# Masked cross attention on one NeuronCore: next-stage loads moved forward, small row transfers moved to another queue, and half of the mask additions moved from TensorE to VectorE

## The reference

```python
x = x + tanh(g_xattn[0]) * L0_attention(layernorm(x), ctx)         # attention over heads, token by token
x = x + tanh(g_ffn[0])   * L0_ffn(layernorm(x))                    # quantised feed-forward
# the stage that is changed: 16 heads of 16, queries from x, keys and values from ctx
q = layernorm(x); query = LN(q @ Wq + bq); key = LN(ctx @ Wk + bk); value = LN(ctx @ Wv + bv)
scores = einsum('bhqd,bhkd->bhqk', query, key) / sqrt(16)
scores = where(mask == 0, -1e9, scores)                            # mask is (8, 512, 512), 0 or 1
probs  = softmax(scores, axis=-1)
x = x + tanh(g_xattn[1]) * (einsum('bhqk,bhkd->bqhd', probs, value) @ Wo + bo)
x = x + tanh(g_ffn[1])   * L1_experts(layernorm(x))                # 8 experts, the best 2 for each token
```

## Time and profile before

| what | value |
|---|---|
| median of 3 runs | 2364.2 us (2363.41 to 2366.39) |
| time of the profiled execution | 2363.78 us |
| its span, first to last instruction | 2362.0 us |
| mean granted clock of PE | 0.905 |
| first_layer, from 0 to about | 553.5 us |
| cross_attention before unit 0, from there to | 682.8 us |
| units 0 to 127, from there to about | 1480 us |
| experts and the end, to | 2362.0 us |

### The profile page before, as it was taken

How to read it: one execution, slowest core, us unless ns; L and a number is a source line. 1 busy time by engine, 2 the same in 40 slices (tenths; PEclk the granted TensorE clock), 3 DMA queues, 4 the chain that set the end, 5 groups by cost and what they waited for, 6 DMA issues and landing times. The chain is left out here.

```text
span 2362.0 us, 35706 instructions
## 1 busy us (share of the span) xinstructions
PE 1962.9 (83%) x12086; PEld 1390.9 (59%) x12086; DVE 1570.8 (67%) x3184; ACT 1078.0 (46%) x2055; POOL 927.8 (39%) x679
## 2 busy tenths in 40 slices
PE   5888898875277989889898979710799999999998
PEld 3566666663123434333343424610799999999998
DVE  7999999973165656556565655450577777777775
ACT  2233334432234555546454545210465655656654
POOL 6988888852432323323232200137222222222222
PEclk8899999987678999999999989655899999999999
DMA  8000000001516345261615320242466666666662
GB/s 291 32 10 10 10 7 10 8 0 56 96 43 96 69 62 90 44 103 32 100 55 77 74 35 2 72 146 100 152 222 224 213 224 225 216 227 226 221 214 73
DMA packets 145296, 245.79 MB, mean 104 GB/s; under 512 B 12613, under 2 KB 90530, under 8 KB 145189
## 3 DMA queue, kind: packets, MB, share of 16 engines
q1 hardware_dynamic: 134540, 219.18, 35.1%
q0 software_dynamic: 10624, 25.26, 2.9%
q10 hardware_dynamic: 24, 0.01, 0.0%
HBM read 201.96 MB, written 45.76 MB: 105 GB/s over the span
## 5 line engine op out<-in xcount | busy, mean ns | idle before, releaser
L1267 DVE CUSTOM_DVE_ANT_0 x_dump<-x_ps,x_bias_q 128x512 bf16<-128x512 f32 x512 | 353.4, 690 | 198.4 <-PE x_ps L1020 185.1
L1171 ACT ACTIVATE x_PT<-x_ps 128x512 f32<-128x512 f32 x512 | 296.1, 600 | 262.9 <-PE x_ps L1035 253.5
L1034 PE MATMUL x_ps<-x_bias_k,x_ident_b 128*128 128x512 bf16 x512 | 200.9, 392 | 75.7 <-DMA x_QS<-x_rows 75.7
L1020 PE MATMUL x_ps<-x_KS,x_QS 96*128 96x512 bf16 x512 | 203.6, 400 | 30.8 <-DMA x_KS<-parts 19.3
L1787 ACT ACTIVATE e_silu<-m_ps 128x256 f32<-128x256 f32 x312 | 118.5, 380 | 232.8 <-PE m_ps L1724 232.7
L1691 POOL DMA_INDIRECT out_dram<-e_y,e_label x78 | 79.0, 1012 | 367.2 <-DVE e_y L1843 355.4
L1035 PE MATMUL x_ps<-x_QS,x_KS 98*128 98x512 bf16 x512 | 200.2, 391 | 0.0
L1826 DVE TENSOR_TENSOR e_gated<-e_silu,m_ps 128x256 f32<-128x256 f32 x312 | 120.8, 417 | 103.0 <-ACT e_silu L1787 98.5
L1724 PE MATMUL m_ps<-e_x_lo,m_hi 128*128 128x256 f32 x640 | 181.4, 283 | 1.5 <-DVE e_x_lo L1811 1.5
L1724 PE MATMUL m_ps<-e_x_hi,m_lo 128*128 128x256 f32 x640 | 181.4, 283 | 0.0
L1724 PE MATMUL m_ps<-e_x_hi,m_hi 128*128 128x256 f32 x640 | 181.1, 283 | 0.0
(11 more groups left out here) (285 smaller groups left out, 5517.7 us busy)
## 6 DMA issues: line engine op xcount, KB each, us to landing
m_raw<-in_L_ffn_w_dram SPq DMA_DIRECT2D x117, 1024.0 KB, 5.1
parts<-x_part SPq DMA_DIRECT2D x24, 512.0 KB, 2.9
x_QS<-parts SPq DMA_DIRECT2D x48, 256.0 KB, 12.0
x_KS<-parts SPq DMA_DIRECT2D x48, 256.0 KB, 16.5
expert_in<-a_blank SPq DMA_DIRECT2D x1, 10062.0 KB, 28.4
e_x<-expert_in SPq DMA_DIRECT2D x39, 258.0 KB, 5.8
x_mask_q<-in_mask_dram SPq DMA_DIRECT2D x32, 256.0 KB, 2.8
x_mask_k<-in_maskT_dram SPq DMA_DIRECT2D x32, 256.0 KB, 2.7
```

Source lines behind the costliest of these rows:

```text
L1020: pe.matmul(ps_max[m % 2], QS[b % 2][0:HROWS, h, q * P:(q + 1) * P], KS[b % 2][0:HROWS, h, :], start=True, stop=True).then_inc(s1_ps, 1)
L1034: pe.matmul(ps_st[e % 3], ident_b[:, :], bias_k[b % 2][:, kc, :], start=True, stop=False)
L1171: act.activation(PT[unit % 2][:, k, :], ps_st[e % 3], ACT.Exp, scale=DH ** -0.5).then_inc(exp_done, 1)
L1267: dve.tensor_tensor_reduce(out=dump[:, :], in0=ps_max[m % 2], in1=bias_q[b % 2][:, q, :], scale=1.0, scalar=NEG, op0=ALU.add, op1=ALU.max, ...
```

## The change

In first_layer, SP also loads the second attention's weights, scales, first two context tiles and first two mask tiles, and DVE splits its biases into three parts in round 33 of 39; all go to tiles that live through both stages (Ahead). In cross_attention:

- the loads of the weights and the bias split at the start are gone; FIRST_UNIT is -16, and start_of is two units later (4n - 28). The first four tiles have their own full and rest (in PT), and DVE does their scale_and_shift, remainder and low_part;
- the extra rows are placed by ACT's own queue, one unit later; the spreading is cut in two: the first two of eight pairs of heads, with a count of their own (first_in), then the rest; SP waits for a given rows transfer before it spreads;
- the first two heads of each group get no mask matmul (CUT = 2). After the second maximum of each unit, DVE takes the minimum of the two exponentials of the unit before and of (mask bias + 2^100), in one instruction on 128 x 1024 elements, and PE's values wait for it (cut_masked);
- once a batch, PE adds up the mask biases of all keys in ps_m, and DVE corrects the bias of those queries that keep no key (keys): one operation on 128 x 512 and four more that add to the four bias tiles; the maximum is bounded to match (NONE_KEPT).

```diff
+            for n in range(2):
+                sp.dma_start(ahead.cT[n][:, :, :], cv[:, :, n * P:(n + 1) * P]).then_inc(ahead.loaded, 16)
+            sp.dma_start(ahead.wkv[:, :, 0:D], k2(L1[2])).then_inc(ahead.loaded, 16)
...
+                if t == NT + 1:
+                    split_biases(7, next_row, next_rest, next_parts)
...
+            def place_rows(g):
+                b = g // GROUPS
+                act.wait_ge(rows_sb, g + 1)
+                heads = slice(4 * (g % GROUPS), 4 * (g % GROUPS) + 4)
+                for r in range(MROWS):
+                    act.dma_start(QS[b % 2][HROWS + r:HROWS + r + 1, heads, :], rows[4 * r:4 * r + 4, :]).then_inc(rows_in, 16)
...
                     if k == 0:
+                        if group_at(unit + 1) is not None:
+                            place_rows(group_at(unit + 1))
...
+                        if b:
+                            sp.wait_ge(rows_in, 16 * MROWS * (rows_before_spread(b) + 1))
                         for part in range(3):
-                            spread_part(b, part)
+                            spread_part(b, part, slice(0, 2), first_in)
+                        for part in range(3):
+                            spread_part(b, part, slice(2, H // 2), spread_in)
...
                 if i == 0:
+                    pe.wait_ge(first_in, 16 * 2 * PARTS * (b + 1))
+                elif i == 16:
                     pe.wait_ge(spread_in, 16 * 2 * PARTS * (b + 1))
...
-                if u == 0 and k == 0:
-                    pe.wait_ge(k_masked, TPB * (b + 1))
+                if u == 0 and k == CUT:
+                    pe.wait_ge(m_free, m_freed["keys", b])
...
-                pe.matmul(ps_st[e % 3], ident_b[:, :], bias_k[b % 2][:, kc, :], start=True, stop=False)
+                if k >= CUT:
+                    pe.matmul(ps_st[e % 3], ident_b[:, :], bias_k[b % 2][:, kc, :], start=True, stop=False)
                 pe.matmul(ps_st[e % 3], KS[b % 2][:, h, kc * P:(kc + 1) * P], QS[b % 2][:, h, :],
-                          start=False, stop=True).then_inc(st_ready, 1)
+                          start=(k < CUT), stop=True).then_inc(st_ready, 1)
...
                 pe.wait_ge(exp_done, 4 * (unit + 1))
+                pe.wait_ge(cut, unit + 1)
...
+                elif what == "keys":
+                    for kc in range(TPB):
+                        mm = pe.matmul(ps_m, ones_b[:, :], bias_k[n % 2][:, kc, :], start=(kc == 0), stop=(kc == TPB - 1))
...
+            def keys(b):
+                dve.wait_ge(m_ready, m_use["keys", b] + 1)
+                steps.done(dve.tensor_scalar(ps_m, ps_m, SEQ * NEG, NONE_KEPT - NEG, ALU.is_equal, ALU.mult))
+                steps.wait()
+                for kc in range(TPB):
+                    d = dve.tensor_tensor(bias_k[b % 2][:, kc, :], bias_k[b % 2][:, kc, :], ps_m, ALU.add)
+                d.then_inc(m_free, 1)
+
+            def cut_masked(unit):
+                b, u = divmod(unit, UNITS)
+                if u == 0:
+                    dve.wait_ge(m_free, m_freed["keys", b])
+                dve.wait_ge(exp_done, 4 * unit + CUT)
+                out = PT[unit % 2][:, 0:CUT, :]
+                dve.scalar_tensor_tensor(out=out, in0=bias_k[b % 2][:, u % TPB, :].unsqueeze(1).broadcast_to([P, CUT, SEQ]),
+                                         scalar=-NEG, in1=out, op0=ALU.add, op1=ALU.min).then_inc(cut, 1)
...
                 for m in islice(maxima, 2):
                     maximum(m)
+                if 0 <= unit - 1 < NUNITS:
+                    cut_masked(unit - 1)
                 for n in tiles_at(unit - 1):
                     kv_stats(n)
...
+                if unit == FIRST_UNIT + 4:
+                    dve.wait_ge(ahead.loaded, AHEAD)
+                    for n in range(EARLY):
+                        scale_and_shift(n)
+                        if n > 1:
+                            remainder(n - 2)
+                    for n in range(EARLY - 2, EARLY):
+                        remainder(n)
+                        low_part(n - 2)
+                    for n in range(EARLY - 2, EARLY):
+                        low_part(n)
```

More of the change, by code:

```diff
@@ L2 @@
 from concourse import mybir
+from collections import namedtuple
 from contextlib import ExitStack
@@ L640 @@
 NEG = -2.0 ** 100
+NONE_KEPT = NEG + 2.0 ** 92
+CUT = 2
 PARTS = 6
@@ L649, with middles_at, rows_before_spread @@
 Q_PARTS, K_PARTS = (0, 0, 1, 1, 0, 2), (0, 1, 0, 1, 2, 0)
-FIRST_UNIT, LAST_UNIT = -18, NUNITS + 5
+FIRST_UNIT, LAST_UNIT = -16, NUNITS + 5
 def start_of(n):
-    return FIRST_UNIT if n < EARLY else 4 * n - 30
+    return FIRST_UNIT if n < EARLY else 4 * n - 28
 def split_of(n):
-    return FIRST_UNIT + 4 + n if n < EARLY else start_of(n) + 4
+    return start_of(n) + 4
+def middles_at(unit):
+    return [n for n in range(NT) if split_of(n) + (1 if n < EARLY else 2) == unit]
 def spread_of(b):
-    return split_of(TPB * b + TPB - 1) + 3
+    return split_of(TPB * b + TPB - 1) + (3 if b else 1)
+def rows_before_spread(b):
+    return (spread_of(b) + 1) // 4
 def tiles_at(unit):
@@ L701, in bank_m_events @@
         late.append(("spread", group_at(unit - 6)))
+    if (unit + 1) % UNITS == 0 and 0 <= unit + 1 < NUNITS:
+        late.append(("keys", (unit + 1) // UNITS))
     if group_at(unit + 2) is not None:
@@ L796, in cross_attention @@
                     m_use[e], m_before[e], last = len(m_use), last, e
-                    if e[0] in ("spread", "output"):
+                    if e[0] in ("spread", "keys", "output"):
                         m_freed[e] = len(m_freed) + 2
@@ L972, in _ @@
                     q_deviations(n)
-                if unit == FIRST_UNIT + 4:
+                if unit == FIRST_UNIT + 2:
                     x_deviations(1)
@@ L1093, in _ @@
                         scores(unit, k)
-                    if k == 1:
+                    if k == (1 if unit >= 0 else 3):
                         for n in tiles_at(unit - 2):
@@ L1229, in split_bias, with part_at, scale_and_shift, remainder @@
                 dve.tensor_tensor(part(2), remainder, part(1), ALU.subtract).then_inc(bias_split, 1)
+            def part_at(n, k):
+                return parts[0][k][:, :, :, n * P:(n + 1) * P].rearrange("p k c n -> p (k c) n")
+            def scale_and_shift(n):
+                dve.wait_ge(turned, n + 1)
+                for k in range(4):
+                    d = dve.tensor_scalar(full(n)[:, k, :], bank_of(n)[:, k * P:(k + 1) * P], scale4[:, k:k + 1], shift4[:, k:k + 1],
+                                          ALU.mult, ALU.add)
+                d.then_inc(full_done, 1)
+            def remainder(n):
+                dve.wait_ge(hi_done, n + 1)
+                dve.tensor_tensor(rest(n), full(n), part_at(n, 0), ALU.subtract).then_inc(rest_done, 1)
+            def low_part(n):
+                dve.wait_ge(mid_done, n + 1)
+                dve.tensor_tensor(part_at(n, 2), rest(n), part_at(n, 1), ALU.subtract).then_inc(lo_done, 1)
             def normalise(n):
@@ L1330, in _ @@
                         divide(n)
+                    elif what == "keys":
+                        keys(n)
                     elif what == "output":
                         output(n)
-                if unit == FIRST_UNIT + 3:
+                if unit == FIRST_UNIT + 2:
                     x_stats(1)
+                if unit == FIRST_UNIT + 4:
+                    dve.wait_ge(ahead.loaded, AHEAD)
+                    for n in range(EARLY):
+                        scale_and_shift(n)
+                        if n > 1:
+                            remainder(n - 2)
+                    for n in range(EARLY - 2, EARLY):
+                        remainder(n)
+                        low_part(n - 2)
+                    for n in range(EARLY - 2, EARLY):
+                        low_part(n)
                     dve.wait_ge(rstd_done, 2)
```

212 lines of the change are left out of this document (111 added, 101 removed).

## The result

The changed kernel takes 2421.1 us, median of 4 runs (2418.76 to 2425.35); the kernel before took 2365.3 beside it on the same chip. The ratio is 1.0235, 95% interval 1.0214 to 1.0256. So the change costs 56 us, where 22 were forecast. The profiled execution took 2425.35, its span is 2423.6, so span against span the difference is 61.6 us.

What follows compares the result with a forecast made beforehand. A batch was taken as PE's, with DVE having 40 us to spare on average. Terms -43 + 1 - 81 + 3 + 78 - 1 + 10 + 3 + 24 + 28 gave +22: 2364.2 to 2386 us, range 2344 to 2422.

Steps and rivals of the forecast that it cites:

- start, with the bias split: Before unit 0: earlier loads, own tile buffers and less spreading to await give -43; bias split in first layer +1.
- rows: stall gone, what is left late: Seven PE stalls before units needing rows: -76, slower matmuls behind them -5, remaining lateness +3.
- backlog: Four-unit cycles: DVE's statistics and other work delay the first maximum, +0.4 a cycle over 26 cycles, +10 (0 to 40).
- rival 3: The stall stays: rows still queue in the transfer engines, half of 76 comes back, 2424 us; chance 0.06.
- I add 3: Rows on ACT's queue: lateness left after the later issue, +3 (0 if always landed, 10 if spreading slows it).
- The cut: PE-DVE-PE loop of plain units: 4.40 instead of 3.76 us, +78 over 122 units; about -1 in the last six.
- The port: Cut and POOL shut each other out of SBUF in a cycle's second and third units: +28 (0 to 60).
- The keys: Once a batch, five DVE operations (3.2 us) before the next unit's first maximum: 8 x 3.0, +24 (16 to 28).
- Rival 1: POOL is never in the cut's way: the port's 28 go, start at -48, rows on time, 2350; chance 0.22.
- Rival 2: PE loses its clock (1 a batch, +8) and port waits reach 2.3 a cycle (+30): 2424 us; chance 0.10.
- Rival 4: The cut is hidden, plain units 3.76 or less, so 78 + 10 + 28 go: 2270 us; chance 0.06.
- no wait of PE for the rows beyond 1 us: Sign expected in the profile after: PE never waits over 1 us for the extra rows.

Runs made afterwards that it cites:

- run 3: Changed kernel with the extra rows issued as soon as they are copied, a unit earlier, still on ACT's queue: 2402.1 us.
- run 9: Changed kernel with the rows back on SP's queue, issued two units ahead as in the kernel before: 2411.5 us.
- run 10: Kernel without keys, with spreading in four paced steps, early rows on ACT's queue, new start and the cut of two heads: 2350.9 us.
- run 11: Changed kernel with one head cut instead of two (CUT = 1): 2379.9 us.
- run 4: Changed kernel with the cut after all maxima of its own unit instead of between the maxima of the next: 2413.2 us.
- run 8: Changed kernel with POOL beginning its operations in each unit only when that unit's cut is over: 2406.5 us.
- run 2: Changed kernel without the keys event (no sums of mask biases on PE, no bias correction on DVE): 2392.9 us.
- run 6: Changed kernel with the spreading from the second batch on in four paced steps of 12 smaller transfers: 2379.9 us.
- run 7: Changed kernel without cut and keys, with paced spreading, early rows and a bound of the maxima that never acts; new start kept: 2229.0 us.

## Why the prediction came out wrong in size

The direction held, and so did the mechanisms of the start, the cut, the port and the keys; that of the rows did not. The sum was 34 short of the medians' difference. By terms, from unit starts, span against span:

| term | forecast | measured | from |
|---|---|---|---|
| start, with the bias split | -42 | -38 | unit 0 at 644.6, before 682.8 |
| rows: stall gone, what is left late | -78 | -41 | seven units and the ones behind them: 84.0 before, 43.2 after |
| all else in the loop (cut, backlog, outputs, keys, port, last units) | +142 | +142 | units 0 to 127: 100.7 longer, plus the 41 |
| end | 0 | -1 | after unit 127 |
| sum | +22 | +62 | span 2423.6 against 2362.0 |

**The rows: the step that failed.** "On ACT's queue they no longer stand behind the spreading: -76, and -5 for the slower matmuls behind seven stalls", with the 3 for lateness, was mis-sized by half; 41 came, not 78. The mechanism behind it, that a queue of one's own lets a small transfer pass, gives almost nothing here (runs 3 and 9). The prediction had drawn on the Trainium skill (DMA: Bandwidth & Descriptors, Queues, rings and completion order) for it, and the measurement does not agree: 8 KB on ACT's ring took 8.9 us with the spreading in flight, with no packet moved for the first 7.7 of them, and came when SP's own next tile came. This is rival 3 ("half of 76 comes back: 2424"), which was given 0.06 on the words "another ring". The rows of the trace had more to say. In the kernel before, the rows reached PE 31.0 after the first issue of the spreading. The change makes SP wait for the rows of unit 8 before it begins, and 31 us do not fit into four units of 22 to 26: 31 - 26 is the 5 of each stall. That sum was to be made and was not. "I add 3" priced a single small transfer, without what else is in flight, and even its upper end, "10 if the rest of the spreading slows it", is a quarter of the 43 that were left.

**The cut.** 78 - 1 + 10 + 3 + 28 = 118 was forecast, the port included, and run 10 measures 122. The two parts err in opposite directions: the port is under its 28 (below), so the rest of the cut is above its 90. That the table's third row agrees to a microsecond is partly luck. The loop of a plain unit was followed step by step: 4.46 to 4.50 against 4.40, by the cut's hand-over (0.15 instead of 0.07). Run 11 confirms that it goes by length, and run 4 that it goes by place. DVE's 1.22 alone was exact.

**The port.** The two units of a cycle were named rightly, and the two that are free of it. The size is 20.7 of longer cuts instead of 28, and 15 by removal (run 8). The lock itself, which the Trainium skill (SBUF — State Buffer, Who interferes with whom) also states, is shown in both directions: the cut is longer beside POOL, and POOL's mask piece beside the cut.

**The keys.** 24 forecast, 28 by run 2, and 29 between runs 6 and 10 (which differ by the early rows too). The trace shows more than DVE's 3.2 in most batches, because PE's clock falls behind the gap: unit 16 is 4.66 longer and unit 15 0.88.

**The start.** 38 of 42.

**The loops without bias and keys** got 5 us shorter in sum (run 7 against before, from unit 0 to 127 without stalls), perhaps for the early projections and turned rows; no run tests it. The prediction had this only as a part of the backlog. 122 + 28 - 5 gives 145 for the 142 of the table.

**Rival 1** fell with run 8. **Rival 2** asked for a port wait of 2.3 a cycle and 1 a batch for the clock. Run 8 gives the port 0.85 a cycle. The clock does fall behind stalls and keys' gaps (0.92 in the window of a batch, 0.95 before), and no run separates what that costs. **Rival 4** is out: plain units went from 3.76 to 4.50. The time 2424 that two rivals gave is close to the 2421 measured, and it came about by rival 3.

**What would have shown it.** Of the signs listed, "no wait of PE for the rows beyond 1 us" was the one that failed, and it pointed straight at the term.

## What to carry to other kernels

When a small transfer is late behind a large one, another queue is not the cure unless a trace shows that it passes. Price it by when the large one is through, counted from what starts it, and send the large one in pieces between the small ones' deadlines; here the smaller pieces and the pauses gave 41 us together. A stage with one fixed-time chain beside the loop (30 us for every four units) takes back what is won in the loop, so that removing one cost (61) and its true price (122) differ by half. Measure a part's price in a kernel where nothing else waits. And an instruction on an engine that is idle on the average is not free if its place is inside the loop between two engines: follow one turn of that loop by its starts.

## What was not expected of the hardware

- Rows of 8 KB, issued by ACT 8.9 us before use, arrived together with a tile of SP's queue issued 2.6 us before them (11.1 from issue to landing, alone 2.7). From the first issue of the spreading to their arrival it was 31 us on either queue, and before as after the change.
- Behind a gap of 2 us on PE the next matmuls ran at half the clock for several us: 1.91 instead of 1.05 for the eight of the values, 3.78 for a projection. Now and then the same occurred in a unit without a long gap: unit 22 took 9.16 instead of 7.67, with a granted clock of 0.53 from 807.88 to 815.00.
- With all gaps gone the granted clock of a whole batch was 1.00 (run 7), where 0.95 stood before.
- A three-operand instruction on 1024 elements with f32 and bf16 from SBUF took 1.22 alone and 1.31 to 1.76 beside POOL; on 512 elements 0.69.
- The spreading moved 130 GB/s at a DMA share of 0.51 in transfers of 64 KB (run 6), and 122 GB/s at 1.09 in transfers of 192 KB (the changed kernel). Those of the keys landed 2.8 and 12.5 us after their issue, by the median.
